# A quantised feed-forward stage: the root of the gelus' mean square and "x plus bias" moved to GpSimd, the statistics of the finished rows moved ahead of the levels, and two PSUM copies moved ahead of the squares

## The reference

```python
def simple_rms_norm(x, dim):
    rms = jnp.sqrt(jnp.mean(x * x, axis=-1, keepdims=True) + EPS_RMS)
    return x / rms * dim ** (-0.5)
def activation_quant(x):
    scale = 127.0 / jnp.clip(jnp.max(jnp.abs(x), axis=-1, keepdims=True), EPS_Q)
    return jnp.clip(jnp.round(x * scale), -128, 127) / scale
def weight_quant(w):
    return jnp.sign(w) * jnp.mean(jnp.abs(w))
def bit_linear(x, w, b, dim_in):
    x_q = activation_quant(simple_rms_norm(x, dim_in))
    return jnp.einsum('bsd,od->bso', x_q, weight_quant(w)) + b
h = bit_linear(x, w1, b1, 512)           # 512 -> 2048
h = gelu(h)
y = bit_linear(h, w2, b2, 2048)          # 2048 -> 512
x = layernorm(x + y)
```

## Time and profile before

| | |
|---|---|
| median of 3 runs | 2914.24 us (2910.81 to 2917.01) |
| the profiled execution, its own time | 2908.72 us |
| its span | 2906.9 us |
| busy in the span | TensorE 2467.0 us (85%), VectorE 1799.7 (62%), ScalarE 1248.9 (43%), GpSimd 297.7 (10%) |
| the last stage | about 2617 to 2894 us of the span, then a 12.6 us store of x |
| one middle round (2738.6 to 2766.9) | 28.3 us: TensorE busy 19.98, VectorE 25.14, ScalarE 17.41, GpSimd 6.91; granted TensorE clock 0.86 |

### The profile page before, as it was taken

One profiled execution on the slowest core, in us unless ns is written; L12 is line 12 of the kernel. 1 busy time (PEld: TensorE's weight loads), 2 busy tenths in 40 slices (PEclk: granted clock), 3 DMA queues, 4 the chain that ended last, 5 costly groups with the idle time before them and its releaser, 6 DMA issues. The chain is left out here.

```text
span 2906.9 us, 42566 instructions
## 1 busy us (share of the span) xinstructions
PE 2467.0 (85%) x15730; PEld 1904.7 (66%) x15746; DVE 1799.7 (62%) x5199; ACT 1248.9 (43%) x2982; POOL 297.7 (10%) x535
## 2 busy tenths in 40 slices
PE   5889999999974999799999999995888888883674
PEld 4668999998864999476667766763655555551332
DVE  6656767667875666445445544454566666657986
ACT  3434445444433211244344434452544444436663
POOL 3211100001000000000000000002111111101220
PEclk8999999999986999999999999997999999996887
DMA  4101211112005000000000000001000000003001
GB/s 156 62 23 41 70 37 40 69 36 74 29 26 194 1 1 1 1 1 1 1 1 1 1 1 1 1 1 51 5 5 5 5 5 5 5 1 133 1 1 58
DMA packets 41212, 83.41 MB, mean 29 GB/s; under 512 B 4528, under 2 KB 17840, under 8 KB 39856
## 3 DMA queue, kind: packets, MB, share of 16 engines
q1 hardware_dynamic: 41008, 80.70, 7.9%
HBM read 72.30 MB, written 8.39 MB: 28 GB/s over the span
## 5 line engine op out<-in xcount | busy, mean ns | idle before, releaser
L1990 DVE TENSOR_REDUCE s_nmax<-s_a_ps 128x2 f32<-128x512 f32 x256 | 174.3, 686 | 198.7 <-PE s_a_ps L1772 195.7
L651 ACT ACTIVATE s_p<-s_ms,s_nmax 128x256 f32<-128x256 f32 x256 | 128.5, 503 | 192.3 <-DVE s_nmax L754 192.3
L754 DVE CUSTOM_DVE_ANT_0 s_ms<-s_s_ps,s_bias 128x256 f32<-128x256 f32 x256 | 98.2, 421 | 175.9 <-PE s_s_ps L529 175.5
L1375 ACT ACTIVATE l_wo_w<-l_wo_w,s_nmax 128x128 f32<-128x128 f32 (+1 forms) x256 | 114.4, 447 | 197.8 <-DVE s_nmax L1471 197.0
L512 PE MATMUL s_q_ps<-s_xT,s_wh 128*128 128x256 f32 x1024 | 189.6, 286 | 0.0
L1215 PE MATMUL s_s_ps<-l_wqb_w,s_lT 128*128 128x512 f32 x384 | 175.7, 597 | 16.0 <-DVE l_wo_w L1441 15.3
L914 PE MATMUL s_h_ps<-s_xh,s_t 128*128 128x256 f32 x704 | 173.0, 284 | 9.3 <-DVE s_xl L1002 9.3
L1886 ACT ACTIVATE s_pT<-s_s_ps 128x512 f32<-128x512 f32 x256 | 151.6, 606 | 59.6 <-PE s_s_ps L1785 57.3
L562 PE MATMUL s_y_ps<-s_wh,s_oT 128*128 128x512 f32 x512 | 173.0, 399 | 0.0
L914 PE MATMUL s_h_ps<-s_xl,s_t 128*128 128x256 f32 x704 | 172.4, 283 | 0.0
L512 PEld LDWEIGHTS s_q_ps<-s_xT,s_wh 128*128 128x128 f32 x1024 | 165.5, 193 | 6.0 <-issue 0.5
(11 more groups left out here) (304 smaller groups left out, 6686.8 us busy)
## 6 DMA issues: line engine op xcount, KB each, us to landing
s_x_raw<-kept SPq DMA_DIRECT2D x24, 512.0 KB, 3.3
s_c_in<-in_ctx_T SPq DMA_DIRECT2D x32, 256.0 KB, 2.5
l_wqb_w<-in_l_xwq SPq DMA_DIRECT2D x4, 1024.0 KB, 7.8
l_wqb_w<-in_l_xwo SPq DMA_DIRECT2D x4, 1024.0 KB, 10.1
kept<-s_x_raw SPq DMA_DIRECT2D x8, 512.0 KB, 2.7
l_wo_w<-in_l_wo SPq DMA_DIRECT2D x1, 4096.0 KB, 15.5
s_raw<-in_l_w1T SPq DMA_DIRECT2D x2, 2048.0 KB, 9.9
s_raw<-in_l_w2T SPq DMA_DIRECT2D x2, 2048.0 KB, 21.5
```

The costliest lines, as they stand in the source:

```text
L651: act.activation(p[:, h % PR, q, :], ms[:, h % 2, q, :], ACT.Exp, scale=-1.0, bias=nmax[:, h % PR, q:q + 1], accum_out=den[:, h % PR, q:q ...
L754: dve.tensor_tensor_reduce(ms[:, h % 2, q, :], s_ps[:, h % 2, q * S:(q + 1) * S], bias[:, h // PER % B, :], -SCALE, 3.0e38, ALU.add, ALU.m ...
L1375: act.activation(p[:, h % PR, q, 0:(q + 1) * P], ms[:, h % 2, q, 0:(q + 1) * P], ACT.Exp, scale=-1.0, bias=nmax[:, h % PR, q:q + 1], accum ...
L1990: dve.tensor_reduce(nmax[:, g % 2, :, 2 * pair + e], a_ps[:, n % 2, :].rearrange("p (q k) -> p q k", q=QT), AX_X, ALU.max, negate=True).th ...
```

## The change

All of it is in the last stage.

- `inverse_root` on the gelus' mean square (12 tiny operations on VectorE) becomes `root_of_h` on GpSimd: 15 tiny operations (the scaling of the squares, the first guess, three Newton steps of four operations each in `root_refine`, the final factor). VectorE keeps the five operations for the levels and waits for GpSimd's root ahead of them.
- x plus b2 is formed on GpSimd (`joined`) into `r`, after x of the last batch is written; VectorE then adds y times unit to it in one operation. L2368 goes, and so does the copy `unit_last` (L2335).
- On VectorE, y times unit plus `r` and the statistics of batch b-1 come ahead of the levels of batch b, and its `row_scales` comes ahead of the clamp of the rounded gelus. The rounding of the next x stands after the fourth of the eight evictions, not after the eighth.
- On ScalarE the copies `hqT` of q = 1 stand ahead of the two squares.
- On GpSimd the clamp of the next x comes first in a round, then the root, then `joined`.

```diff
@@ scalar, round_of
+                for use in late:
+                    rows_over(a_turns.at(b, use), a_turns.bank(b, use), *use[1:])
                 if has(b, "here"):
                     act.wait_ge(g_full, b * QT + QT)
                     for q in range(QT):
                         act.activation(sq[:, :], h[:, q, :], ACT.Square, accum_out=hs["squares"][:, q:q + 1]).then_inc(sq_full, 1)
                         act.wait_ge(sq_full, b * QT + q + 1)
-                for use in late:
-                    rows_over(a_turns.at(b, use), a_turns.bank(b, use), *use[1:])
@@ gpsimd
+            def root_of_h(b):
+                pool.wait_ge(sq_full, b * QT + QT)
+                core.apart(pool)
+                root.round(b)
+                root.done(pool.tensor_scalar(hs["squares"][:, :], hs["squares"][:, :], 1.0 / INNER, EPS_RMS, ALU.mult, ALU.add))
+                root_refine_start(root)
+                root.done(pool.tensor_scalar(hs["root"][:, :], hs["root"][:, :], float(np.float32(INNER ** -0.5)), None, ALU.mult))
+                root.end()
+            def joined(b):
+                if b > 0:
+                    pool.wait_ge(dve_steps, b * LN_STEPS)
+                    core.apart(pool)
+                xb_of = core.x[:, b * QT:(b + 1) * QT, :]
+                pool.tensor_tensor(r[:, :, :], xb_of, b2_sb[:, :].unsqueeze(1).broadcast_to([P, QT, D]), ALU.add).then_inc(xb_full, 1)
...
             x_bounded(0)
-            x_bounded(1)
-            for b in range(2, B):
-                x_bounded(b)
+            pool.wait_ge(b_full, 16)
+            for b in range(B):
+                if has(b, "next"):
+                    x_bounded(b + 1)
+                root_of_h(b)
+                joined(b)
@@ vector, round_of
-                if has(b, "prev"):
-                    last_steps.round(b - 1)
-                    last_steps.done(dve.tensor_copy(unit_last[:, :], hs["unit"][:, :]))
...
+                        if n == IC - 1 and has(b, "next"):
+                            x_rounded(b + 1)
-                if has(b, "next"):
-                    x_rounded(b + 1)
...
                     here_steps.done(dve.tensor_reduce(hs["most"][:, :], h[:, :, :], AX_X, ALU.max, apply_absolute_value=True))
-                    dve.wait_ge(sq_full, b * QT + QT)
-                    scales(here_steps, hs, INNER)
+                if has(b, "prev"):
+                    last_steps.round(b - 1)
+                    dve.wait_ge(xb_full, b)
+                    for q in range(QT):
+                        dve.wait_ge(y_full, (b - 1) * QT + q + 1)
+                        dve.scalar_tensor_tensor(out=r[:, q, :], in0=y_ps[:, q, :], scalar=hs["unit"][:, q:q + 1],
+                                                 in1=r[:, q, :], op0=ALU.mult, op1=ALU.add).then_inc(y_out, 1)
+                    dve.wait_ge(y_out, b * QT + QT)
+                    row_statistics(core, last_steps, dve, r, w)
+                if has(b, "here"):
+                    dve.wait_ge(root_steps, (b + 1) * ROOT_OF_H)
+                    levels_of_h(here_steps)
```

More of the change, by code:

```diff
@@ L2283, in _, with root_refine_start @@
             pool.sem_inc(xq_full, QT)
-            x_bounded(0)
-            x_bounded(1)
-            for b in range(2, B):
-                x_bounded(b)
+            def root_of_h(b):
[6 more added lines that the diff above has]
+                root.end()
+            def root_refine_start(step):
+                v, y = hs["squares"][:, :], hs["root"][:, :]
+                step.done(pool.tensor_scalar(y.bitcast(I32), v.bitcast(I32), -0.5, RSQRT_MAGIC, ALU.mult, ALU.add))
+                root_refine(step, pool, v, y, hs["tmp"][:, :])
+            def joined(b):
[4 more added lines that the diff above has]
+                pool.tensor_tensor(r[:, :, :], xb_of, b2_sb[:, :].unsqueeze(1).broadcast_to([P, QT, D]), ALU.add).then_inc(xb_full, 1)
+            root = Steps(pool, root_steps, ROOT_OF_H)
+            x_bounded(0)
+            pool.wait_ge(b_full, 16)
[4 more added lines that the diff above has]
+                joined(b)
         @block.vector
@@ L2329, in x_rounded, with levels_of_h @@
                                       ALU.mult, ALU.add).then_inc(xw_full, 1)
+            def levels_of_h(step):
+                step.done(dve.tensor_tensor(hs["most"][:, :], hs["most"][:, :], hs["root"][:, :], ALU.mult))
+                step.done(dve.tensor_scalar(hs["most"][:, :], hs["most"][:, :], EPS_Q, None, ALU.max))
+                step.done(dve.reciprocal(hs["levels"][:, :], hs["most"][:, :]))
+                step.done(dve.tensor_scalar(hs["levels"][:, :], hs["levels"][:, :], 127.0, None, ALU.mult))
+                step.done(dve.tensor_tensor(hs["levels"][:, :], hs["levels"][:, :], hs["root"][:, :], ALU.mult))
             def round_of(b):
-                if has(b, "prev"):
-                    last_steps.round(b - 1)
-                    last_steps.done(dve.tensor_copy(unit_last[:, :], hs["unit"][:, :]))
                 if has(b, "here"):
@@ L2340, in round_of @@
                         dve.scalar_tensor_tensor(out=h[:, q, c], in0=v_ps[:, n % IC, :],
-                                                 scalar=xs["unit"][:, bass.ds(b * QT + q, 1)], in1=b1_sb[:, c],
+                                                 scalar=xs["unit"][:, b * QT + q:b * QT + q + 1], in1=b1_sb[:, c],
                                                  op0=ALU.mult, op1=ALU.add).then_inc(v_out, 1)
-                if has(b, "next"):
-                    x_rounded(b + 1)
-                if isinstance(b, int) and b == 0:
+                        if n == IC - 1 and has(b, "next"):
+                            x_rounded(b + 1)
+                if b == 0:
                     magnitudes(1)
-                    dve.wait_ge(b_full, 16)
                 if has(b, "here"):
@@ L2359, in round_of @@
                     here_steps.end()
[L2360 to L2364, removed]
-                if has(b, "prev"):
[L2366 to L2370, removed]
+                if has(b, "prev"):
+                    row_scales(last_steps, dve, w)
                 for q in range(QT):
```

9 lines of the change are left out of this document (4 added, 5 removed).

## The result

The changed kernel takes 2891.9 us in the median of four runs (2886.94 to 2892.9), the kernel before 2913.09 beside it: a ratio of 0.9926, 95% interval 0.9914 to 0.9938, faster by 21.2 us.

The account below looks back on a forecast made before the run. No engine full; two nearly equal chains of waits across engines bound each 28.37 us round. Terms summed to 26.2, plus 0.6 gave 26.8: 9.4 over six periods plus 3.0 in round 0, 12.4 off 2914.24: 2901.8, range 2894 to 2909.

Parts of the forecast that it names:

- the first term of the sum: Gelus up to the maximum's start: 7.76 us after the first eviction, plus 0.6 allowed for a slower TensorE product.
- round 1's row: TensorE's first product of q = 1 took 6.58 us after 3.65 idle, 1.89 of transposes and 0.80 idle.
- TensorE no slower: Rival: TensorE as in round 3, no allowance, period 26.2, gain 16.0, 2898.2 us; chance 0.13.
- TensorE comes late: Rival: colder TensorE slows its products, period 27.3 or 27.4, 2905 us, or 2908.5 with both; chance 0.23.
- Copies and squares: ScalarE's q = 1 copies and two squares after the gelus: terms of 1.95 and 4.06 us in the round's sum.
- The end: After round 7: first clamp 1.3 us later, vanished sum gives back 1.28, net 0.
- Sums and statistics under the wait for the root: VectorE's sum (1.41 us) and statistics (1.7) leave the path, hidden while GpSimd's root runs until 18.0.
- the danger named: VectorE operations from SBUF to SBUF stand during GpSimd's addition; roundings of x at risk, losing about 0.2 us if late.
- Rounding x in the middle: VectorE's 0.87 us rounding after four evictions costs nothing, as it waits there for the first product's last chunks.
- The cost of this edit is none: GpSimd's addition of x plus b2, 2.34 to 2.40 us beside VectorE's evictions, is free unless ports are shared.
- A slow root: Rival: GpSimd's fifteen root steps take 7.3 us rather than 4.13, total 2924 us, slower than before; chance 0.04.
- the change hides nothing: Rival: evictions stand still for GpSimd, up to 5 us a round; with smaller mishaps about 2907 to 2912; chance 0.05.

Follow-up runs that it names:

- a_fill: Changed kernel plus 22 extra matmuls, never read, on TensorE ahead of the transposes of q = 0 in rounds 1 to 7: 2892.36 us.
- u_join: Changed kernel with x plus b2 back on VectorE instead of GpSimd: 2901.02 us.
- n_free: Kernel of n_hold without the hold, so GpSimd adds x and b2 as soon as the rows are written: 2905.3 us.
- u_round: Changed kernel with x rounded after the eighth eviction again: 2901.67 us.
- u_scales: Changed kernel with the row scales behind the clamps again: 2904.24 us.
- u_root: Changed kernel with the root of the mean square back on VectorE, twelve tiny operations ahead of the levels: 2904.86 us.
- n_hold: Changed kernel with row scales directly behind the statistics, rows scaled between the clamps, GpSimd's addition held until both clamps are done: 2890.47 us.
- a_short: Changed kernel plus only 8 extra matmuls, shrinking TensorE's idle stretch ahead of the transposes: 2895.45 us.
- n_fill: n_hold plus extra matmuls in rounds 2 to 7, 19 ahead of the transposes of q = 0 and 4 behind them: 2884.65 us.

## Why the prediction was wrong in size

*The step that failed* is the first term of the sum: "I allow 0.6, half of the difference of 1.12: period 26.8". I took the maximum to start at 7.76 + 0.6 = 8.36. It started at 7.3. That is 1.0 of the 1.3 us by which each period came out shorter, 6 of the 9.5 us by which the span's gain (21.9) exceeded the sum (12.4). Two things were wrong in it. I did not look for a floor: in the kernel before the maximum starts 2.30 later than the product is long (5.46 and 7.76, 6.58 and 8.88), but in round 4, with 4.97, it was at 7.32, and a_fill shows that it stays at 7.32 however quick TensorE is. And I read round 1's row as a pattern (idle, transposes, idle, slow product) that the new order would repeat. In the changed kernel the transposes behind 5.3 to 6.1 us of idling took 1.89 from round 2 on, at the lower clock, directly ahead of the product, which then took 4.1 to 5.2 and stayed under the floor or passed it by 0.1. My rival "TensorE no slower" used 7.76 and was too timid as well. That the product would be quicker I did not foresee, and why its slow time fell as it did is open; that it fell under the floor was luck as far as the forecast goes.

One argument for "TensorE comes late" was misread as well: "every part that followed an idle of 3 us was slow" holds for the earlier trace rows, but behind the same idle of 3.19 the second part took 3.63 in rounds 1, 2 and 5.

*The other terms.* Copies and squares took 5.7 from the start of the maximum, not 1.95 + 4.06, since the copies start 0.14 before it and the squares follow them without a gap. The clamp took 1.21 on the path, not 1.32. The two waits around the root took 0.3 together, not 0.1. All this is 0.3 a round, 1.7 in all, the rest of the periods' surplus of 7.8. Root 4.09 against 4.13, levels 1.00, scaling and unit 2.66, row scales 2.17: all as worked out. Round 0 gave 3.3 against 3.0. The end gave 0.65 against 0: the first clamp of round 7 came 0.9 later, not 1.3. The 0.8 ahead of the stage belongs to no edit, and other runs of unchanged code there differ by more.

*What hid where.* Sums and statistics under the wait for the root: confirmed, VectorE waited up to 2.1 us for GpSimd. GpSimd's addition free beside the evictions: confirmed, 0.75 an eviction, as without it in u_join; and n_free shows that the danger named was real one place further on. Rounding x in the middle "costs nothing": true, but I missed that it pays, 1.5 a round in u_round, most of it by starting GpSimd's clamps early. "The cost of this edit is none" for x plus b2: it pays too, 1.0 a round in u_join, 0.87 of it because no addition of two SBUF operands runs beside the root any more.

*The rivals.* TensorE late, at 0.23, did not come in the changed kernel, and came in u_scales, u_root, u_round and n_hold. A slow root did not come: 0.275 a step. Nor was an eviction or a rounding of x stretched, as "the change hides nothing" would have had it.

*The range* had its low end from a run spread of 3 us around a fast case that was not the fastest possible. Undoing single parts costs 1.0 to 4.0 a round, 10.7 summed over five parts, where all together brought 2.9: no sum over parts could have told the whole. These prices include what TensorE's clock did in each run. The sixth part, sums and statistics ahead of the levels, was not undone by itself, so its price is not shown.

## What to carry to other kernels

Before allowing for a variable engine, find the floor that another engine sets, and take the fast case from there. In a round that crosses engines, a wait placed on a steady engine (here GpSimd's root) can be worth more than a quiet round shows (1.1 us against 0.4), because it absorbs the lateness of an unsteady one that ends ahead of it. When two engines slow each other at SBUF, look for the pairs that a change separates, not only for those it creates.

## What the runs showed of the hardware

TensorE's clock after an idle stretch of 3.6 to 4.8 us followed no rule of idle time alone. What these rounds show is an exchange. In n_hold, always behind 4.8 us of idling, transposes of 1.89 us had a product of 4.6 to 4.8 behind them, shorter ones (1.57 to 1.79) one of 5.8 or 5.9. In a_short, transposes at the lower clock (1.88 to 1.89 us) had a product of 4.2 or 5.1 behind them, transposes at the upper (1.07) one of 5.0 or 6.5. In the kernel before, a first product of 5.8 to 6.6 had a quick second part of the second product in the same round (3.63), one of 5.0 to 5.7 a slow one (5.31). It is no rule either: in u_root transposes of 1.89 behind 6.4 us of idling had a product of 5.7 behind them.

In u_root, with periods of 27.30, the product was the same in each round to 0.02 us, while in the changed kernel, with 25.5, it alternated from round 2 on between 4.1 to 4.3 and 5.0 to 5.2 us. I read this as decisions of the clock that keep a time of their own, against which a kernel's rhythm falls in or out of step; no run here shows the decisions themselves. "TensorE: Matmul & The Clock Gate" (Part 1) of the Trainium skill says that the monitor runs freely and that the same kernel therefore changes clock at varying places; these runs agree in that equal rounds of one kernel ran at different clocks, with products of 4.2 and 5.1. With the idle stretches filled (n_fill) the granted clock was 1.00. That kernel's 5.8 us against n_hold's median come from matmuls whose results nobody reads.
